# Values times key features: two 128x128 products become four products on 64-column halves of the array

## The reference

```python
q, k, v = heads(x @ Wq + bq), heads(x @ Wk + bk), heads(x @ Wv + bv)   # 16 heads of 16
q, k = features(q), features(k)            # exp(x - max) / (sum + EPS)
numerator = einsum('bhld,bhmd->bhlm', q, k)
probs = numerator / (sum(q, -1) + EPS)
context = einsum('bhlm,bhmd->bhld', probs, v)
x = layernorm(x + context @ Wo + bo)
x = layernorm(x + fp4_linear(silu(fp4_linear(x, w_gate)) * fp4_linear(x, w_up), w_down))
```

## Time and profile before

| | |
|---|---|
| time, median of 3 runs (lowest to highest) | 763.99 us (763.69 to 764.46) |
| the profiled execution's own time | 763.37 us |
| its span, first to last instruction | 761.6 us |
| TensorE busy | 718.2 us, 94% |
| VectorE, ScalarE, GpSimd busy | 616.5, 581.2, 559.8 us (81, 76, 73%) |
| share of TensorE in the chain that ended last | 84% |
| mean granted TensorE clock | 0.982 of full |

### The profile page before, as it was taken

The page is one execution under the profiler, slowest core; times in us unless marked ns, Lnnn a source line. Parts: engine busy times, 40 slices in busy tenths (PEclk is TensorE's granted clock), DMA queues, the critical chain, the costliest instruction groups (busy, mean ns, idle before and its releaser), DMA issues.

```text
span 761.6 us, 17047 instructions
## 1 busy us (share of the span) xinstructions
PE 718.2 (94%) x4964; PEld 687.4 (90%) x4964; DVE 616.5 (81%) x1402; ACT 581.2 (76%) x1547; POOL 559.8 (73%) x585
## 2 busy tenths in 40 slices
PE   4999999999999968699999999999999999999983
PEld 3899999999999857699999999999999999999983
DVE  5988788889888985788878878788799887898773
ACT  3577776777898887468887877767777788888887
POOL 4677677677667675758887878878888788787761
PEclk9999999999999988799999999999999999999998
DMA  4222222222222110000000000000000001111113
GB/s 131 70 67 75 83 76 72 71 65 77 78 69 77 49 28 1 1 1 2 1 2 1 2 1 2 2 2 1 1 1 2 15 29 44 43 43 36 49 64 131
DMA packets 39767, 29.80 MB, mean 39 GB/s; under 512 B 3446, under 2 KB 39676, under 8 KB 39676
## 3 DMA queue, kind: packets, MB, share of 16 engines
q1 hardware_dynamic: 37228, 26.50, 11.5%
q10 hardware_dynamic: 2448, 2.23, 1.1%
HBM read 20.32 MB, written 8.39 MB: 38 GB/s over the span
## 4 chain that ended last, share of the span: by engine, by line
PE 84%; issue 5%; DVE 4%; POOL 3%; ACT 2%; DMA 1%; ACTq 0%; SPq 0%; POOLq 0%; DVEq 0%
PE bank L856 63%; PE wide L856 5%; PE wide L959 5%; PE bank L918 3%; PE bank L864 3%; PE bank L916 2%; PE bank L966 2%; PE wide L905 2%; POOL scratch L387 1%; ACT scratch L488 1%; POOL scratch L373 1%; DMA scratch<-L_attn_Wv 1%; PE wide L892 0%; POOL scratch L430 0%; POOL scratch L423 0%
## 5 line engine op out<-in xcount | busy, mean ns | idle before, releaser
L856 PE MATMUL bank<-wf_hi,rounded 128*128 128x352 f32 (+1 forms) x1792 | 405.1, 311 | 14.2 <-DVE wf_lo L739 6.1
L856 PEld LDWEIGHTS bank<-wf_hi,rounded 128*128 128x128 f32 x1792 | 302.7, 191 | 17.5 <-DVE wf_lo L739 6.3
L856 PE MATMUL bank<-wf_lo,rounded 128*128 128x352 f32 (+1 forms) x896 | 275.2, 307 | 0.0
L856 PEld LDWEIGHTS bank<-wf_lo,rounded 128*128 128x128 f32 x896 | 171.4, 191 | 0.0
L430 POOL TENSOR_TENSOR scratch<-scratch 128x704 f32<-128x704 f32 x64 | 94.9, 1482 | 78.5 <-DVE scratch L812 75.1
L856 PE MATMUL bank<-qkv_hi,rounded 128*128 128x512 f32 (+1 forms) x512 | 145.9, 339 | 0.0
L415 POOL TENSOR_TENSOR scratch<-scratch 128x704 bf16<-128x704 f32 x64 | 99.3, 1551 | 14.5 <-ACT scratch L609 14.0
L856 PEld LDWEIGHTS bank<-qkv_hi,rounded 128*128 128x128 f32 x512 | 93.3, 191 | 9.9
L781 DVE TENSOR_TENSOR scratch<-scratch,bank 128x352 f32<-128x352 f32 x64 | 33.2, 519 | 72.2 <-ACT scratch L566 70.1
L435 POOL TENSOR_TENSOR scratch<-scratch 128x704 f32<-128x704 bf16 x64 | 89.0, 1390 | 0.7 <-DVE scratch L816 0.7
L373 POOL TENSOR_TENSOR scratch<-scratch 128x512 f32<-128x512 f32 x64 | 68.0, 1063 | 27.8 <-DVE scratch L726 27.5
(11 more groups left out here) (100 smaller groups left out, 1578.2 us busy)
## 6 DMA issues: line engine op xcount, KB each, us to landing
scratch<-x_feat SPq DMA_DIRECT2D x64, 128.0 KB, 2.2
scratch<-x_tok SPq DMA_DIRECT2D x64, 128.0 KB, 2.1
out<-scratch SPq DMA_DIRECT2D x64, 128.0 KB, 1.7
scratch<-w_ffn ACTq DMA_DIRECT2D x17, 128.0 KB, 2.2
scratch<-L_attn_Wq SPq DMA_DIRECT2D x1, 256.0 KB, 3.0
scratch<-L_attn_Wk SPq DMA_DIRECT2D x1, 256.0 KB, 3.1
scratch<-L_attn_Wv SPq DMA_DIRECT2D x1, 256.0 KB, 3.9
wo<-L_attn_Wo SPq DMA_DIRECT2D x1, 256.0 KB, 3.1
```

The source lines that it names most:

```text
L856: last = pe.matmul(dst, x(c), w(c), start=first and n == 0, stop=n == len(terms) - 1)
```

## The change

Each 128x128 product of a chunk becomes two: values of features `k` to `k+63` of the chunk (stationary, 128 tokens x 64) times the key features of the same 64 (streamed, 64 columns), for `k` = 0 and 64. The first is placed on columns 0 to 63 of the array and writes PSUM partitions 0 to 63, the second on columns 64 to 127 with partitions 64 to 127. The two blocks that lie off the diagonal (features of the first half against those of the second) are not computed. `pkv` is then 64 columns to a chunk, so VectorE's masking runs as two instructions of 64 partitions and 2x64 elements in place of one of 128 partitions and 256 elements. What they don't write of `kv_m` is set to zero once, at the start, on GpSimd.

```diff
+KVW = 64
...
                 pool.memset(prob[b][:, NH:, HD:], FEPS)
+            pool.memset(kv_m, 0.0)
             pool.memset(ident[:, :], 0.0).then_inc(consts, 1)
...
-                        dve.tensor_tensor(kv_m, pkv[:, 0:KC * P].rearrange("p (c n) -> p c n", c=KC),
-                                          mask[:, :, :], ALU.mult).then_inc(a_kvm, 1)
+                        for k in range(0, P, KVW):
+                            at = slice(k, k + KVW)
+                            op = dve.tensor_tensor(kv_m[at, :, at],
+                                                   pkv[at, 0:KC * KVW].rearrange("p (c n) -> p c n", c=KC),
+                                                   mask[at, :, at], ALU.mult)
+                        op.then_inc(a_kvm, 1)
...
                         for c in range(KC):
-                            last = pe.matmul(pkv[:, c * P:(c + 1) * P], v_sb[b][:, c * P:(c + 1) * P],
-                                             feat[b][:, D + c * P:D + (c + 1) * P],
-                                             start=s == 0 and c == 0, stop=s == T - 1, skip_group_check=True)
+                            for k in range(0, P, KVW):
+                                at = slice(c * P + k, c * P + k + KVW)
+                                last = pe.matmul(pkv[k:k + KVW, c * KVW:(c + 1) * KVW], v_sb[b][:, at],
+                                                 feat[b][:, D + at.start:D + at.stop], start=s == 0 and c == 0,
+                                                 stop=s == T - 1, skip_group_check=True, tile_position=(0, k))
                         last.then_inc(a_post, 1)
```

## The result

The changed kernel takes 770.75 us (median of 4, 770.62 to 771.91) against 763.84 (763.37 to 764.46); the ratio is 1.0093, 95% interval 1.0076 to 1.0111. That is +6.9 us. I had forecast 755.

What follows compares the result with a forecast made beforehand. The prediction took a full TensorE in the attention as the bound. From 763.37 us it summed -10.4 (overlap) + 1.5 (others following) + 0.2 (masking) + 0 (memset) = -8.7, to 754.7, about 755; range 751 to 781.

Steps and rivals of the forecast that it cites:

- What bounds the kernel: In the attention, 20 to 262 us, TensorE is busy 241.62 of 242 us, so its work goes straight into the time.
- Columns and time, and the overlap: Line 918's products: 64 columns take 0.056 us, halves overlap, block 0.28 for 0.45 us; 0.17 us saved a step, 10.4 in all.
- that rival: Line 918's weight loads don't shrink: eight at 0.11 us each, +0.43 us a step, +26 us, 790; chance 0.09.
- one half after the other: Products or loads don't overlap across halves: the block stays 0.45 us, no change, 763 to 766 us; chance 0.17.
- The switch: Going to half width and back on TensorE, twice a step: bounds nothing to 0.45 us for two, taken near nothing.
- my upper bound: Cost of a width change on TensorE: 0.165 us to empty the array plus 0.06 exposed load, 0.225 each, 0.45 for two.
- the switch eats it: Array drains at both width changes of a step: 0.285 us less 0.17 overlap, +0.115 a step, +7 us, 771; chance 0.30.
- Can the others follow: Other engines keep up with steps of 3.66 us, but VectorE may be late in some: 1.5 us given back.
- 0.74 us of slack for line 746: Low part of `c` is done at 215.89 and wanted at 216.63 us; the slack would shrink to 0.57.
- Masking and memset: VectorE's masking pair +0.04 us, covered except the last, +0.2 us taken; GpSimd's memset, 0.25 us, covered and costing nothing.

Runs made afterwards that it cites:

- exchanged loops: Changed kernel with its two loops exchanged, all products on columns 0 to 63 of the array first, then all on 64 to 127: 770.78 us.
- same half: Changed kernel with all four products of a step on columns 0 to 63 of the array: 781.68 us.
- full-width probe: Kernel before plus one product per step streaming 64 columns, its stationary operand all 128 columns, into unused columns of the bank: 774.76 us.
- half-width probe: Kernel before plus one product per step of 64 values x 64 key features on array columns 64 to 127, result unread: 788.11 us.
- grouped runs: Products of several tiles in one go: four tiles on halves 765.96 us, four at full width 772.12; two tiles with one masking instruction, halves 762.87, quarters 756.65.
- pairs of halves: Changed kernel with one masking instruction and the half-width products of two tiles in one go, every second step: 762.87 us.
- The parts alone: Kernel before with only masking in two instructions of 64 partitions and the memset of kv_m, TensorE's products as before: 764.98 us.

## Why the prediction was wrong

**What bounds the kernel**: right in the main. TensorE is full in the attention, and the attention's trace is 6.9 us longer, the whole loss. Of these 5.9 us are TensorE's own and 1.0 us comes from the masking. 61 steps of +0.11 us give nearly the same number, 6.7, which is in part chance: the undisturbed step grew by 0.12, and some late steps, in which TensorE waits for VectorE, by less.

**Columns and time, and the overlap**: the direction was right, the term was mis-sized. I had 0.17 us saved a step, from starts in the order of issue; it is 0.225, the four matmuls of a half at 0.056 us, whatever the order of issue (exchanged loops, same half). The 0.056 us itself was right with some luck: I had it from the streamed columns alone, and at full width a product that streams 64 columns still costs 0.105 us. What went with it was the weight load, whose columns were halved too; that this is the cause is inferred from the full-width probe. The load shrinks with the columns, 138 against 192 ns, so that rival fell. So did the rival of one half after the other (781.7 on one half, 770.75 on two).

**The switch**: this is the step that failed; I had put it at nothing. "The likeliest case for me is overlap with a switch near nothing, because I find no gap in this trace at any of the switches that it does have." None of those changed the width, as I wrote beside it, and the argument was worth nothing. With its 0.34 us the step's saving of 0.225 us turns into a loss of 0.11. Measured: 0.34 us for both, by the changed kernel and again, 0.33, by the half-width probe, within the bounds that I had from rows (0.12 to 0.45) and near their middle, 0.285. Of the two parts of my upper bound, the wait for the product ahead was 0.09 us a switch and not 0.165, and the exposed load 0.05 us on the way in and 0.10 on the way out and not 0.06. The rival *the switch eats it*, to which I gave a chance of 0.30 against 0.44 for a switch that costs nothing, gave 771, with +0.115 us a step; measured are 770.75 and +0.11. Its saving was too small by 0.055 and its price by the same amount, so the agreement is better than its terms. The rule that the page "TensorEngine Tiling (Array Packing)", Key Properties, of the Trainium skill states, that changing the tiling mode drains TensorE, agrees with this case's traces: the first load at the new width waits 0.17 us, and the new width starts 0.07 us before the recorded end of the last product, however long that one is.

**Can the others follow**: not tested by the change, since steps grew. The grouped runs show it was a fair question: with pairs of halves, 764.42 - 762.87 = 1.6 of the forecast 3.5 us came through against the runs of before beside it. My reading of 0.74 us of slack for line 746 was that of one sequence. It holds for ten of the 16; in the others the trace of before has 0.27, 0.24 and 0.65 us, and in the last three TensorE already waits.

**Masking and memset**: +0.04 us a pair was mis-sized; 0.53 against 0.36 us is +0.17. The parts alone cost 1.2 us, not 0.2. I had called the price covered by looking at one stretch, 207 to 217 us. In four sequences a VectorE that is 0.1 us late makes the low part of `c` up to 0.6 us late, and TensorE waits for it. The memset was covered as forecast: VectorE's third instruction starts at 6.38 us in the run with the parts alone, at 6.36 before.

## To carry to other kernels

Placing products on halves or quarters of the array really does run them side by side, but each change of width around them costs about 0.17 us of a full TensorE here, as much as six 64-column matmuls on two halves (0.17 / 0.028). Count the switches, not the products: gather what is narrow into long runs (with one masking instruction, two tiles at a time turned a loss of 0.8% into a gain of 0.2% with halves; with quarters the gain was 1.0%), yet no longer than leaves the steps even for the engines that feed it. Slack that is read in one place holds for that place: look for the steps where it is smallest. And where a trace shows no instance of a transition, its absence of gaps elsewhere is no price; take the middle of the bounds, or measure it with a probe.

## What I had not expected of the hardware

Matmuls of the two halves don't wait for each other in the order of issue: four and four in a row took as long as in alternation (eight starts within 0.24 and 0.23 us). The records don't name the half; that the starts come in pairs 14 and 7 ns apart, where one half alone never has two within 0.058 us, is the evidence. At full width a float32 product that streams 64 columns costs as much as one that streams 128 (0.105 and 0.11 us), while at half width it costs 0.056: narrowing only the streamed side would have gained next to nothing. The price of a switch hardly depends on what stands ahead of it, since the new width starts 0.07 us before the recorded end of the last product in all five cases of the table. And the array took 16 matmuls of 32 columns within 0.13 us, so issue is far from being a bound here.
